# A mixture-of-experts block on one core: the residual and the expert rows are added up in DRAM, and the scratch table goes

## The reference, cut to what matters

```python
x = x + attention(layernorm(x))                       # 16 x 128 tokens of 256 values
x = x + cross_attention(layernorm(x), ctx)
t = layernorm(x).reshape(2048, 256)
logits = silu(t @ rw1 + rb1) @ rw2 + rb2              # router, 8 experts
w = softmax(the two largest logits of each token)     # the others are 0
eh = silu(einsum('td,edh->teh', t, ew1) + eb1)
eo = einsum('teh,ehd->ted', eh, ew2) + eb2
return x + t + einsum('te,ted->td', w, eo)
```

## Time and profile before

| what | us |
|---|---|
| median of 3 runs | 585.55 (584.58 to 586.25) |
| span of the profiled execution | 586.8 |
| barrier between the two phases | 387.8 |
| first gather, first scatter start | 407.25, 424.38 |
| last scatter starts, has landed | 570.01, 572.35 |

### The profile page before, as it was taken

How to read it: one execution, slowest core, us unless ns; L and a number is a source line. 1 busy time by engine, 2 the same in 40 slices (tenths; PEclk the granted TensorE clock), 3 DMA queues, 4 the chain that set the end, 5 groups by cost and what they waited for, 6 DMA issues and landing times. The chain is left out here.

```text
span 586.8 us, 11994 instructions
## 1 busy us (share of the span) xinstructions
PE 483.2 (82%) x3828; PEld 335.3 (57%) x3829; DVE 368.2 (63%) x841; ACT 272.9 (47%) x692; POOL 179.8 (31%) x152
## 2 busy tenths in 40 slices
PE   1999889999999999899999887330998888888860
PEld 1555489555588555598555675230765655555540
DVE  5844775847675937675845679878544554445564
ACT  5355373255464355462455578243444344343430
POOL 0301240402140401330410223324456554555440
PEclk9999999999999999999999999755799999999995
DMA  8501001000001010000000624200121222212608
GB/s 334 193 0 37 1 1 38 1 3 34 37 0 36 0 36 20 16 0 0 0 0 38 259 85 160 71 31 26 52 67 57 64 62 64 70 64 59 212 13 286
DMA packets 15450, 37.05 MB, mean 63 GB/s; under 512 B 2877, under 2 KB 9166, under 8 KB 14272
## 3 DMA queue, kind: packets, MB, share of 16 engines
q1 hardware_dynamic: 10336, 25.14, 11.9%
q0 software_dynamic: 3744, 9.47, 5.4%
q10 hardware_dynamic: 1344, 2.10, 0.9%
HBM read 28.24 MB, written 9.37 MB: 64 GB/s over the span
## 5 line engine op out<-in xcount | busy, mean ns | idle before, releaser
L825 PE MATMUL pj<-up_h,up_f 128*128 128x512 f16 x480 | 111.4, 385 | 6.3 <-ACT down L317 3.0
L1274 ACT ACTIVATE hT<-h,b 128x128 f32<-128x128 f32 x156 | 44.6, 368 | 91.7 <-remote 65.7
L825 PEld LDWEIGHTS pj<-up_h,up_f 128*128 128x128 f16 x480 | 45.7, 99 | 64.1 <-ACT down L317 6.8
L1520 PE MATMUL h<-xt,up_h 128*128 128x128 f16 x624 | 73.0, 223 | 3.9 <-issue 3.4
L1520 PEld LDWEIGHTS h<-xt,up_h 128*128 x624 | 52.7, 100 | 25.7 <-issue 11.5
L410 ACT ACTIVATE p<-sc,nm 128x128 f32<-128x128 f32 x128 | 45.4, 375 | 45.7 <-DVE nm L738 45.7
L1520 PE MATMUL h<-xt,up_l 128*128 128x128 f16 x312 | 62.4, 223 | 4.7 <-issue 4.7
L264 POOL TENSOR_TENSOR pn<-p,inv 128x512 f32<-128x512 f32 x32 | 36.4, 1138 | 89.9 <-DVE inv L705 89.9
L1395 DVE COPY xt<-rank 128x512 f16<-128x512 f16 x39 | 16.5, 422 | 73.9 <-remote 66.3
L1229 POOL DMA_INDIRECT picked<-ys,dst_row x39 | 40.2, 1032 | 63.2 <-DVE ys L1409 54.7
L1220 POOL DMA_INDIRECT got<-rows,src_row x39 | 44.9, 1152 | 19.7 <-issue 11.1
(11 more groups left out here) (245 smaller groups left out, 1033.9 us busy)
## 6 DMA issues: line engine op xcount, KB each, us to landing
up_f<-in_ew SPq DMA_DIRECT2D x8, 1024.0 KB, 5.0
up_f<-picked SPq DMA_DIRECT2D x6, 512.0 KB, 6.3
rows<-row SPq DMA_DIRECT2D x4, 528.0 KB, 2.7
xg<-in_x SPq DMA_DIRECT2D x4, 512.0 KB, 3.5
up_l<-in_ctx SPq DMA_DIRECT2D x4, 512.0 KB, 4.9
v<-in_w SPq DMA_DIRECT2D x2, 1024.0 KB, 9.3
down<-in_w SPq DMA_DIRECT2D x1, 1024.0 KB, 12.2
down<-in_wc SPq DMA_DIRECT2D x1, 1024.0 KB, 14.7
```

The lines of the kernel that those rows point to most:

```text
L825: last = pe.matmul(out, w(c), v(c), start=(i == 0), stop=(i == len(terms) - 1))
L1274: last = act.activation(hT[s][:, m, :], hb[s][:, m * P:(m + 1) * P], ACT.Silu, bias=b1[:, bass.ds(e * MC + m, 1)], scale=DOWN)
L1520: ins = pe.matmul(hb[s][:, m * P:(m + 1) * P], lhs, xt[s][:, x, :], start=(j == 0), stop=(j == 3 * KC - 1))
```

## The change

Four things are done in another way:

1. The result tensor gets 128 spare rows behind its 2048, cut off by the host. `base` shrinks to one group; SP writes it to the result in DRAM after each group (`base_out` counts these stores), and DVE waits for the store before it overwrites the buffer.
2. Rows are numbered in natural order (sequence times 128 plus partition), in `rows` too. The sign and the instructions that make it and take it off again are gone; a padding slot gets the spare row of its partition.
3. The scatter of a tile adds its rows to the result in DRAM (`compute_op=ALU.add`). Since a token occurs in two tiles, and adding is a read and a write, each scatter waits until the scatter before has landed; the first waits for the four base stores as well.
4. `picked`, its reads, the additions and the final writes are gone, with the count `early` that told when the first half of the reads may begin.

```diff
+            sp.sem_inc(base_out, 16)
...
             def rows_of(g):
+                sp.wait_ge(base_done, g + 1)
+                sp.dma_start(out_t[g], base[:]).then_inc(base_out, 16)
                 sp.wait_ge(wrow2, g + 1)
                 sp.dma_start(rows_t[g], row[:].bitcast(U32)).then_inc(row_out, 16)
...
+            sp.wait_ge(base_done, G + 1)
+            sp.dma_start(out_t[G - 1], base[:]).then_inc(base_out, 16)
...
                 dve.wait_ge(ln[3]["xn"], r + 1)
-                dve.scalar_tensor_tensor(out=base[:, bass.ds(r * GB, GB), :], in0=xn[:], scalar=1.0 / UP, in1=x2[:],
+                dve.wait_ge(base_out, 16 * r + 16)
+                dve.scalar_tensor_tensor(out=base[:], in0=xn[:], scalar=1.0 / UP, in1=x2[:],
                                          op0=ALU.mult, op1=ALU.add).then_inc(base_done, 1)
...
                 if t == 0:
                     pool.wait_ge(dst_done, 1)
+                    pool.wait_ge(base_out, 16 * G + 16)
+                else:
+                    pool.wait_ge(scattered[(t - 1) % SLOTS], 16 * ((t - 1) // SLOTS + 1))
                 pool.wait_ge(y_free, t + 2)
-                pool.indirect_dma_start(picked, bass.IndirectOffsetOnAxis(dst_row[:, t:t + 1], 0), ys[s][:], None,
-                                        bounds_check=2 * B * L - 1, oob_is_err=False).then_inc(scattered[s], 16)
+                pool.indirect_dma_start(out, bass.IndirectOffsetOnAxis(dst_row[:, t:t + 1], 0), ys[s][:], None,
+                                        bounds_check=B * L + P - 1, oob_is_err=True, compute_op=ALU.add)\
+                    .then_inc(scattered[s], 16)
...
-            pool.tensor_tensor(pay[:], hot_t[:], signed[:].rearrange("p k b -> p (k b)").unsqueeze(2)
-                               .to_broadcast([P, 2 * B, TILES]), ALU.mult).then_inc(pay_done, 1)
+            for k in range(2):
+                pay_k = pool.tensor_tensor(pay[:, k * B:(k + 1) * B], hot_t[:, k * B:(k + 1) * B],
+                                           token.unsqueeze(2).to_broadcast([P, B, TILES]), ALU.mult)
+            pay_k.then_inc(pay_done, 1)
...
-            done(dve.scalar_tensor_tensor(out=mag[:], in0=inv[:], scalar=-1.0, in1=inv[:], op0=ALU.mult, op1=ALU.max))
-            dve.tensor_scalar(src_row[:], mag[:], -1.0, 0.0, ALU.add, ALU.max).then_inc(idx_done, 1)
+            dve.tensor_scalar(src_row[:], inv[:], -1.0, 0.0, ALU.add, ALU.max).then_inc(idx_done, 1)
...
-            for g in range(G):
-                b = slice(g * GB, (g + 1) * GB)
-                dve.wait_ge(z0_in[g], 16)
-                dve.tensor_tensor(z[:, 0, b], z[:, 0, b], base[:, b, :], ALU.add).then_inc(summed, 1)
-            for g in range(G):
-                b = slice(g * GB, (g + 1) * GB)
-                dve.wait_ge(summed, g + 1)
-                dve.wait_ge(z1_in[g], 16)
-                dve.tensor_tensor(z[:, 0, b], z[:, 0, b], z[:, 1, b], ALU.add).then_inc(fin_done, 1)
...
-              "picked": nc.dram_tensor("picked", [2 * B * L, D], F32, kind="Internal").ap()}
...
-    out = nc.dram_tensor("out", [B, L, D], F32, kind="ExternalOutput").ap()
+    out = nc.dram_tensor("out", [B * L + P, D], F32, kind="ExternalOutput").ap()
```

More of the change, by code:

```diff
@@ L167, in attention_phase @@
         wc_hi, wc_lo, bv_full, bc_done, o_hi = (sem(n) for n in ("wc_hi", "wc_lo", "bv_full", "bc_done", "o_hi"))
-        kept, dbg, waited = sem("kept"), sem("dbg"), sem("waited")
+        waited = sem("waited")
         x_t = x.rearrange("(g b) p d -> g p b d", b=GB)
         c_t = ctxt.rearrange("(g b) p d -> g p b d", b=GB)
-        rows_t = rows.rearrange("(p g b) w -> g p b w", b=GB, g=G)
+        rows_t = rows.rearrange("(g b p) w -> g p b w", b=GB, g=G)
+        out_t = out[0:B * L, :].rearrange("(g b p) d -> g p b d", b=GB, g=G)
+        base_out = shared["base_out"]
         block = ctx.enter_context(nc.Block())
@@ L543, in base_half @@
                 dve.wait_ge(ln[3]["xn"], G + h)
-                dve.scalar_tensor_tensor(out=base[:, (G - 1) * GB + bs.start:(G - 1) * GB + bs.stop, :], in0=xn[:, bs],
-                                         scalar=1.0 / UP, in1=x2[:, bs], op0=ALU.mult, op1=ALU.add).then_inc(base_done, 1)
+                if h == 0:
+                    dve.wait_ge(base_out, 16 * (G - 1) + 16)
+                dve.scalar_tensor_tensor(out=base[:, bs], in0=xn[:, bs], scalar=1.0 / UP, in1=x2[:, bs],
+                                         op0=ALU.mult, op1=ALU.add).then_inc(base_done, 1)
             def rows_low_half(h):
@@ L1087 @@
 assert TILES % SLOTS == 0 and STEPS % SLOTS == 0
-SKIP = 8192
 RW = ROW // 2
@@ L1098, in expert_phase @@
     (eb1, eb2, pick_expert) = dram
-    base, eidx, rows, cols, identh, picked = (shared[k] for k in ("base", "eidx", "rows", "cols", "identh", "picked"))
+    eidx, rows, cols, identh = (shared[k] for k in ("eidx", "rows", "cols", "identh"))
     row, ge, gs, g1, g2, m1, m2 = (shared[k] for k in ("row", "ge", "gs", "g1", "g2", "m1", "m2"))
@@ L1136, in expert_phase @@
         hot_t, pay = sb("hot_t", [P, 2 * B, TILES]), sb("pay", [P, 2 * B, TILES], F16)
[L1137 to L1140, removed]
+        spare = sb("spare", [P, 1])
+        inv, iszero, aside, dsum = (sb(n, [P, TILES]) for n in ("inv", "iszero", "aside", "dsum"))
         src_row, dst_row = sb("src_row", [P, TILES], U32), sb("dst_row", [P, TILES], U32)
@@ L1191, in _ @@
             sp.wait_ge(last_row, 1)
-            sp.dma_start(rows.rearrange("(p g b) w -> g p b w", b=GB, g=G)[G - 1], row[:].bitcast(U32))\
+            sp.dma_start(rows.rearrange("(g b p) w -> g p b w", b=GB, g=G)[G - 1], row[:].bitcast(U32))\
                 .then_inc(row_out, 16)
@@ L1195, in _ @@
             sp.dma_start(b2[E:2 * E, :], b2l[:]).then_inc(b2_lo_in, 16)
[L1197 to L1201, removed]
-            for g in range(G):
[L1203 to L1211, removed]
+            for k in range(SLOTS):
+                sp.wait_ge(scattered[k], 16 * (TILES // SLOTS))
         @block.gpsimd
@@ L1323, in _ @@
             dve.tensor_tensor(m2[:], m2[:], g2[:].unsqueeze(2).to_broadcast([P, GB, E]), ALU.mult)
-            done(dve.tensor_tensor(signed[:, 0], sign[:], token, ALU.mult))
-            dve.tensor_scalar(signed[:, 1], signed[:, 0], -1.0, None, ALU.mult)
+            done(dve.tensor_scalar(spare[:], token[:, 0:1], float(B * L), None, ALU.add))
             dve.tensor_tensor(row[:, :, 2 * D:ROW].bitcast(F32), m1[:], m2[:], ALU.add).then_inc(last_row, 1)
```

46 lines of the change are left out of this document (13 added, 33 removed).

## The result

| | us, median of the runs | lowest to highest | profiled span |
|---|---|---|---|
| before | 585.55 (4 runs) | 584.58 to 586.25 | 586.8 |
| after | 610.49 (4 runs) | 608.78 to 611.55 | 607.0 |

A forecast was written before the change was run, and what follows sets the result against it. The pair's 8.1 us period, with "remote" waits on ACT and DVE, was taken as the pace, no engine being full. 586.8 + 13.2 - 8.7 - 0.4 = 590.9 us profiled, 589.6 as median; range 567 to 606.

The forecast's parts named there:

- The chain of scatters: Tile loop: each scatter waits for the previous landing, period 4.18 us against 4.03; last scatter starts 13.2 us later.
- four bounds: Adding scatter's time to landing: 2.34, 3.1, 3.7 or 6.05 us, giving periods of 3.1, 3.9, 4.5 or 6.8.
- The plain landing: Tile loop: a plain scatter lands 2.34 us after its start, read from scatter 38.
- The end: After the last scatter's start: 16.8 us of combine become 8.1 us, POOL's DRAIN plus 0.4; 8.7 us gained.
- In front of the loop: Before the first gather: `mag` 0.21 and the sign 0.2 us saved, `pay` in halves covered by 1.5; together 0.4 gained.
- At nothing: Parts priced at no cost: base instruction and its store wait, last store, smaller rows pieces, removed `picked` reads; padding tiles count as full.
- A: Rival: the addition is nearly free, the loop keeps its pace and the end shrinks; median 580.3 us, chance 0.22.
- B: Rival: the gain at the end is used up, chain period 3.6 to 4.0 us; median 585 us, chance 0.15.
- C: Rival: the new wait spreads POOL's four DMAs, ending "remote" waits; tiles at 3.5 us, median 564 us, chance 0.14.
- D: Rival: the addition is slow, descriptors one after another; period 4.8 to 6.8 us, time 613 to 690, chance 0.10.
- my own case: The forecast itself, the likeliest case: chain period 4.05 to 4.8 us, end 586 to 610, chance 0.39.
- break-even period: Chain period at which loss and gain balance: 4.07 us, a landing of 3.3 us, last scatter starting at 579.1.

The follow-up runs named there:

- run 1: Also written chain_plain: the kernel after with scatters that write their rows instead of adding them, sums left out; 562.6 us beside 585.2 for before, ratio 0.960.
- run 3: The kernel before with adding scatters and no wait between them, the table filled with the residual first and the combine subtracting it once; 569.94 us, ratio 0.975 to before.
- run 2: The kernel before with plain scatters and only the wait for the scatter before added; 577.36 us beside 585.2, ratio 0.987.
- run 5: The kernel after, but past the first five, scatters wait only if their tile is the first of its expert or padding; 582.33 us, ratio 0.996 to before.
- run 6: Also written pool_waits: the kernel after with POOL itself waiting for the last landing before the block ends; 611.86 us in a single run beside 584.3 for before.
- run 7: Waits at experts' borders only, as in run 5, but padding rows skipped and no wait at padding-only tiles; 571.26 us beside 563.9 for before, ratio 1.014.
- run 9: Both kernels unchanged, side by side on one chip: before 564.49 us, after 611.18 us, ratio 1.083.
- run 4: The kernel before with a small unused memset on POOL ahead of each scatter; 578.94 us beside 584.3, ratio 0.989.

## Why the prediction was wrong in its size

- **The chain of scatters: right in its form, mis-sized in one term.** The period was to be time to landing plus restart, 3.4 + 0.77 = 4.18 us. Restart measured 0.8. The step that failed is the landing of an adding scatter, put at 3.4 us: it measured 3.8. The period is 4.62, and 38 x 0.44 = 16.7 us are the whole error of the sum in the profiled execution (16.1, with 0.8 less in front of the loop and 0.1 more at the end). Of the four bounds the third, 4.5, was the near one. The addition costs 3.8 - 2.4 = 1.4 us of landing, and part of it needs no DRAM: POOL takes 1.59 us instead of 1.02 to make the descriptors, 0.57 us. The working took issue time as unchanged and asked only for the data's read. The remaining 0.8 is as large as the read that the narrow view of the DMA engines showed for a gather. So the second bound (plain landing plus 0.8) plus POOL's 0.57 would have given 3.7. That the 0.8 is the read is argued from its size alone. That nothing hides the landing is shown by runs 1 and 3.
- **The plain landing: right by luck.** The 2.34 us under all four bounds are those of scatter 38, whose tile is padding only: in the kernel before its rows are skipped. From 566 to 573 us, where the last three scatters start, the queue of POOL's DMAs moved nothing (0.00 MB); in chain_plain, where padding rows are written, three scatters moved 0.39 MB between 551 and 560 us (packets, MB, share):

```profile
q0 software_dynamic: 144, 0.00, 1.3%
```

```profile
q0 software_dynamic: 143, 0.39, 10.8%
```

  The first two of those three landed in 2.39 and 2.38 us. So a full scatter that isn't late needs the same time, which the trace of before alone did not show.
- **The Trainium skill** (DMA: Bandwidth & Descriptors, Rules for kernel authors) asks for the earlier DMA's semaphore beside an accumulating one; runs 2, 3 and 5 show that this wait is what makes the addition cost. The estimate from its fixed time and rate (Anatomy of one DMA) was 2.3 us for these bytes: the full plain scatters of run 1 agree where they land in 2.4 (their late ones do not, 3.7 to 4.5), and the adding one does not, 3.8. The agreement that the prediction saw, 2.34, was that of a scatter without bytes.
- **The end: right.** 8.1 us from the last scatter's start were said, 8.2 measured. Of its reason one half stands: the DRAIN belongs to the block with the indirect DMAs and is fully in the open. Whether it hangs on the landing, the open point, is answered by run 6: it does not.
- **In front of the loop: right in sum by accident.** 0.4 us were to be won; the first scatter is 1.2 us earlier (423.20 against 424.38). But `pay` already starts 1.07 us earlier (398.46 against 399.53), from ahead of the steps that I counted, and from there to the first gather the kernel after takes 7.93 us against 7.72. The two halves of `pay` last 5.11 us and end at 403.6, not at 403.1, and the table's matmuls wait for them, so `pay` took the place of `hot_r` and used up what `mag` and the sign gave. Nor are the 1.2 us clear of chance: the unchanged kernels' first scatters stood at 424.38 and 423.13 (before) and at 423.20 and 423.86 (after) in their two profiled executions each. "Covered by 1.5 us" was wrong: with `pay` 1.5 longer the cover is gone. POOL's row:

```profile
398.46 5.11 POOL L1228 TENSOR_TENSOR pay<-hot_t,dc 128x624 f16<-128x624 f32 x2 [7.51 <-DVE hot_t L1330]
```

- **At nothing: right for the stores.** The page's DMA issues (count, KB each, us to landing) show 3.0 us for the row pieces against 2.7, and the residual's stores, all of them long before the loop:

```profile
rows<-row SPq DMA_DIRECT2D x4, 528.0 KB, 3.0
...
out<-base SPq DMA_DIRECT2D x4, 512.0 KB, 3.8
```

  The padding tiles that "count as full" cost what was said, a whole period each, but they are four and not three (in run 5 the last four scatters have the wait); run 7 shows that skipping them and their wait saves 9.5 us over the last six spacings.
- **The rivals.** A and B fall with the period. C's mechanism is real, and I had given it 0.14: the wait between the scatters does end most "remote" waits (run 2), and without the addition the whole kernel takes 562.6 us (run 1), near the 564 of C. The loop that it frees runs at 3.2 us, though, and the period of 4.6 takes that back and more. What C rested on, four DMAs of POOL in a row as the releaser, is not enough as a cause: on the chip of run 9 POOL issues scatter, gather, scatter, gather with no gap above 0.83 us (its rows) and nobody waits. D, whose period began at 4.8, isn't it either: 4.62 lies inside my own case, 4.05 to 4.8.
- **The range: a slip in its upper end.** The case reached to a period of 4.8, and by the prediction's own terms that ends at 423.98 + 38 x 4.8 + 8.1 = 614.5 in the profile, 613 as median, not at "610". The range was cut at 606, inside the likeliest case.
- **"The engines could go at about 3.1" was right, and PE is then the bound** (97% busy, run 9). Its other side was missed: the break-even period of 4.07 us holds only on a chip with the late releases. There the last scatter of before starts at 570.0; on the other at 545.2, and with 8.5 us of gain at the end break-even would be (545.15 + 8.5 - 423.1) / 38 = 3.4 us, less than the landing of an adding scatter alone.

Open stays what releases `hT` and `xt` late on some chips. The runs show that it differs from chip to chip, and on one chip depends on how POOL's indirect DMAs are spaced (runs 1 to 4); no run shows the mechanism.

## What to carry to other kernels

A read-modify-write in DRAM that must wait for the one before it turns time to landing, which a pipeline hides, into a period: price it as landing plus restart, and with the descriptors' extra time on the issuing engine, before the work it replaces is counted. Take such waits only where rows can really collide: between experts instead of between tiles was worth 28 us here, and with the padding skipped the kernel came to 571.3 us, still 1.4% above the kernel before beside it. Read the time of a transfer from one that moves what yours will move. When idle time is put down to a releaser outside the program, time the kernel on another chip before building on that pace: here the baseline itself was 564 or 585.

## What the runs showed of the hardware

- An indirect DMA that adds takes POOL 1.59 us instead of 1.02 for 128 rows of 1 KB, and lands in 3.6 to 3.9 us (after, all but a few) instead of 2.4 (chain_plain, with a few of 3.7 to 4.5). A plain one whose rows were all skipped landed in 2.34 (before).
- A block that ended with indirect DMAs on POOL had a DRAIN there that ended 6.4 us after the last descriptors were made (before, after, chain_plain) or, with everything landed, lasted 6.43 (pool_waits). The block without them had one that ended within 0.1 us of POOL's last instruction (before).
- The kernel before took 563.9 and 564.5 us on two chips, 584.3 to 587.8 in four other stretches of runs, at the same granted clock (0.94 to 0.95 in the mean), the difference being late releases on ACT and DVE in the tile loop. On chips that have them an added wait (0.987), an added memset on POOL (0.989) and adding instead of plain scatters (0.975) each made the kernel faster.
- One 128x1248 multiplication on POOL took 3.60 us; the same work as two of 128x624 took 5.11.
